# Mixture of experts: each expert's gate row brought to all partitions by a DMA instead of a bf16 product, and the first layer's products rotated over four PSUM banks

## The reference, cut to what matters

```python
shared = gelu(x @ sW1 + sb1) @ sW2 + sb2                  # one shared expert, 512 hidden units
weights = softmax(x @ gW + gb)                            # 15 experts
topv, topi = top_k(weights, 3)
gated = (one_hot(topi, 15) * topv[..., None]).sum(-2)     # 15 gates per token, 12 of them zero
routed = einsum('ebtd,bte->btd', expert_e(x), gated)      # 15 experts, 256 hidden units each
out = shared + routed + x
```

## Time and profile before

| | value |
|---|---|
| median of three runs | 2175.12 us |
| profiled execution, its own time | 2172.97 us |
| its span in the trace | 2171.2 us |
| PE busy | 1942.1 us, 89% of the span |
| DVE busy | 1490.1 us, 69% |
| ACT busy | 1440.6 us, 66% |
| POOL busy | 1137.4 us, 52% |
| experts' chunks in the trace | 419 to about 891 us |
| all DMA over the span | 29.16 MB |

### The profile page before, as it was taken

The page is one execution under the profiler, slowest core; times in us unless marked ns, Lnnn a source line. Parts: engine busy times, 40 slices in busy tenths (PEclk is TensorE's granted clock), DMA queues, the critical chain, the costliest instruction groups (busy, mean ns, idle before and its releaser), DMA issues. The chain is left out here.

```text
span 2171.2 us, 63152 instructions
## 1 busy us (share of the span) xinstructions
PE 1942.1 (89%) x23942; PEld 1524.2 (70%) x23942; DVE 1490.1 (69%) x3891; ACT 1440.6 (66%) x4147; POOL 1137.4 (52%) x1477
## 2 busy tenths in 40 slices
PE   5899887399999999699969999966999999999898
PEld 2577565166666667466658888854888888888787
DVE  7699658476666555477746666657777777777567
ACT  4588645387777778488857777747666666666542
POOL 5676359377877788545422232207555445444420
PEclk9999969699999999899989999989999999999999
DMA  3000000300000000000010000010000000000101
GB/s 89 9 2 2 8 2 2 94 1 1 1 1 1 1 1 1 11 2 3 2 32 2 2 2 2 2 65 5 2 17 5 15 17 5 15 15 2 53 8 37
DMA packets 32730, 29.16 MB, mean 13 GB/s; under 512 B 5534, under 2 KB 30126, under 8 KB 32174
## 3 DMA queue, kind: packets, MB, share of 16 engines
q1 hardware_dynamic: 23214, 20.93, 3.2%
q10 hardware_dynamic: 9216, 4.20, 0.7%
HBM read 20.92 MB, written 4.19 MB: 12 GB/s over the span
## 5 line engine op out<-in xcount | busy, mean ns | idle before, releaser
L1023 POOL TENSOR_TENSOR ff_hl<-ff_hid,ff_hh 128x512 fp32r<-128x512 f32 x272 | 353.9, 1309 | 115.5 <-ACT ff_hh L1262 109.0
L1877 POOL TENSOR_TENSOR sm_zsum<-sm_zsum,sm_logits 128x512 f32<-128x512 f32 x120 | 154.6, 1288 | 274.5 <-ACT sm_logits L1903 272.8
L1191 DVE TENSOR_TENSOR ff_hid<-ff_p_b,ff_hid 128x512 f32<-128x512 f32 x240 | 164.1, 685 | 157.7 <-ACT ff_hid L1251 157.4
L1251 ACT ACTIVATE ff_hid<-ff_p_h,ff_b 128x512 f32<-128x512 f32 x272 | 185.6, 683 | 49.5 <-PE ff_p_h L1079 48.1
L1920 ACT ACTIVATE sm_sT<-sm_p_s 128x512 f32<-128x512 f32 x128 | 69.5, 595 | 220.5 <-PE sm_p_s L1713 220.5
L1262 ACT ACTIVATE ff_hh<-ff_hid 128x512 fp32r<-128x512 f32 x272 | 170.1, 625 | 40.1 <-DVE ff_hid L1191 38.0
L581 ACT ACTIVATE at_pr<-at_p_s,at_small 128x64 f32<-128x64 f32 x512 | 154.8, 329 | 61.9 <-DVE at_small L469 61.9
L1889 POOL TENSOR_TENSOR sm_logits<-sm_logits,sm_peak 128x512 f32<-128x512 f32 x128 | 163.0, 1295 | 12.7 <-ACT sm_comb L1938 12.1
L1727 PE MATMUL sm_p_l<-g_phi,g_xnT 128*128 128x256 f32 x512 | 142.6, 405 | 26.8 <-ACT sm_logits L1948 25.4
L548 POOL TENSOR_TENSOR at_kblk<-at_kT,at_heads 128x512 f32<-128x512 f32 x128 | 131.8, 1049 | 35.0 <-PE at_p_s L448 23.6
L1077 PE MATMUL ff_p_h<-ff_xh,ff_w1h 128*128 128x512 f32 x272 | 135.0, 496 | 12.3 <-ACT ff_hid L1251 8.5
(11 more groups left out here) (316 smaller groups left out, 5738.5 us busy)
## 6 DMA issues: line engine op xcount, KB each, us to landing
sm_w<-in_w_soft SPq DMA_DIRECT2D x8, 512.0 KB, 3.5
ff_whole<-in_L_ffn_rW SPq DMA_DIRECT2D x30, 128.0 KB, 2.5
early_xs<-in_x ACTq DMA_DIRECT2D x32, 64.0 KB, 1.9
ld_ctx<-in_ctx ACTq DMA_DIRECT2D x32, 64.0 KB, 2.0
x_kept<-early_xs SPq DMA_DIRECT2D x1, 2048.0 KB, 7.4
g_xnT<-x_kept SPq DMA_DIRECT2D x1, 2048.0 KB, 9.2
out_x<-sm_acc SPq DMA_DIRECT2D x8, 256.0 KB, 2.3
g_phi<-in_L_ffn_phi SPq DMA_DIRECT2D x8, 128.0 KB, 2.4
```

The costliest lines, as they stand in the source:

```text
L1023: eng.tensor_tensor(hl[:, q, :], hid[:, q, :], hh[:, q, :].bitcast(F32), ALU.subtract).then_inc(h_split, 1)
L1191: dve.tensor_tensor(h, p_b[e % 2][:, :], h, ALU.mult).then_inc(scaled, 1)
L1251: act.activation(hid[:, slot(u, c), :], p_h[c % 2][:, :], ACT.Gelu, bias=b1[:, c:c + 1]).then_inc(gelud, 1)
L1877: pool.tensor_tensor(z, z, logits[:, j % RING_L, :, :], ALU.add).then_inc(summed, 1)
```

## The change

It has two parts. First, the gates no longer pass through bf16 parts, PE and PSUM. The float32 gates `gT` of a group (15 rows of 512) are stored to a DRAM buffer by the SP queue, and SP then loads, for each expert, its row of 2 KB into all 128 partitions of one of five SBUF slots (`gates`, 256 KB a load). So the product L1068, the transpose and copy of the parts and the last five router steps are gone, the transpose of the gates moves from c = 30 to c = 21, and the multiply on DVE reads its gates from SBUF. SP waits in its own order: for `gT`, for the store, and before each load for the multiplies of the expert five before. Its loads for group 0 stand behind the second piece of weights. The constants lose `c_spread` and `c_identb`. Second, the two PSUM banks so freed go to `p_h`: product c waits for the Gelu of chunk c-4 instead of c-2.

```diff
@@ -945,11 +945,11 @@
+    GR, PH = 5, 4
+    gates_d = nc.dram_tensor("kept_gates", (NE, NT * P), F32, kind="Internal").ap()
...
-        spread = m.sb("spread", [P, NE, P], BF16)
-        identb = m.sb("identb", [P, P], BF16)
...
-        parts = m.sb("parts", [P, 4, P], BF16)
-        partsT = m.sb("partsT", [P, R, N], BF16)
+        gates = m.sb("gates", [P, GR, N])
...
-        p_h = [m.ps(f"p_h{i}") for i in range(2)]
-        p_b = [m.ps(f"p_b{i}") for i in range(2)]
+        p_h = [m.ps(f"p_h{i}") for i in range(PH)]
...
+        def spread_gates(sync, t, experts_of):
+
+            at = slice(t * N, (t + 1) * N)
+            if experts_of[0] == 0:
+                sync.wait_ge(gT_copied, t + 1)
+                sync.dma_start(gates_d[:, at], gT[0:NE, t % R, :]).then_inc(gates_kept, 16)
+                sync.wait_ge(gates_kept, 16 * (t + 1))
+            for e in experts_of:
+                n = NE * t + e
+                if n >= GR:
+                    sync.wait_ge(scaled, CE * (n - GR + 1))
+                sync.dma_start(gates[:, n % GR, :], gates_d[e:e + 1, at].to_broadcast([P, N])).then_inc(gate_in[n % GR], 16)
...
                 for dst, src in piece:
                     sync.dma_start(dst, src).then_inc(w_in[i], 16)
-
-
-        AT_LOGITS, AT_LOGITS_T, AT_PARTS_T, AT_G_T = 1, 3, 26, 30
+                if i == 1:
+                    spread_gates(sync, 0, range(GR))
+            spread_gates(sync, 0, range(GR, NE))
+            for t in range(1, NGR):
+                spread_gates(sync, t, range(NE))
+
+        AT_LOGITS, AT_LOGITS_T, AT_G_T = 1, 3, 21
...
@@ -1057,26 +1071,16 @@
-                        if c >= CS and (c - CS) % CE == 0:
-                            e = (c - CS) // CE
-                            if e == 0:
-                                pe.wait_ge(pT_copied, t + 1)
-                            if e >= 2:
-                                pe.wait_ge(scaled, (NC_FF - CS) * t + CE * (e - 1))
-                            elif live(t - 1):
-                                pe.wait_ge(scaled, (NC_FF - CS) * t)
-                            pe.matmul(p_b[e % 2][:, :], spread[:, e, :], partsT[:, u, :], start=True, stop=True).then_inc(b_done, 1)
-                        if c >= 2:
-                            pe.wait_ge(gelud, NC_FF * t + c - 1)
-                        elif live(t - 1):
-                            pe.wait_ge(gelud, NC_FF * t)
+                        n = NC_FF * t + c
+                        if n >= PH:
+                            pe.wait_ge(gelud, n - PH + 1)
...
-                    if c == AT_PARTS_T and nxt:
-                        pe.wait_ge(parts_ready, t + 2)
-                        for q in range(4):
-                            mm = pe.transpose(p_q[:, :].bitcast(BF16)[:, q * P:(q + 1) * P], parts[:, q, :], identb[:, :])
-                        mm.then_inc(pT_done, 1)
                     if c == AT_G_T and nxt:
-                        pe.wait_ge(pT_copied, t + 2)
+                        pe.wait_ge(r_step, STEPS * (t + 2))
...
@@ -1186,9 +1178,10 @@
                         dve.wait_ge(gelud, NC_FF * t + c + 1)
-                        dve.wait_ge(b_done, NE * t + e + 1)
+                        n = NE * t + e
+                        dve.wait_ge(gate_in[n % GR], 16 * (n // GR + 1))
                         h = hid[:, slot(u, c), :]
-                        dve.tensor_tensor(h, p_b[e % 2][:, :], h, ALU.mult).then_inc(scaled, 1)
+                        dve.tensor_tensor(h, gates[:, n % GR, :], h, ALU.mult).then_inc(scaled, 1)
...
@@ -1266,11 +1259,10 @@
-                    if c == AT_PARTS_T + 1 and nxt:
-                        act.wait_ge(pT_done, t + 2)
-                        act.activation(partsT[:, (u + 1) % 2, :], p_q[:, :].bitcast(BF16)[:, 0:N], ACT.Copy).then_inc(pT_copied, 1)
                     if c == AT_G_T + 1 and nxt:
                         act.wait_ge(gT_done, t + 2)
+                        if live(t - 1):
+                            act.wait_ge(gates_kept, 16 * t)
```

More of the change, by code:

```diff
@@ L959, in experts @@
         loads = [(gw[:, :], io["L0_ffn_gW"]), (gb[:, :], io["L0_ffn_gb"].rearrange("(e a) -> e a", a=1)),
-                 (spread[:, :, :], io["c_spread"].rearrange("p (e m) -> p e m", e=NE)), (identb[:, :], io["c_identb"]),
                  (seg[:, :], io["c_seg"]), (b1[:, :], io["w_b1"]), (b2[:, :], io["w_b2"])]
@@ L985, in experts @@
         s4 = m.sb("s4", [P, 5, 4])
-        parts = m.sb("parts", [P, 4, P], BF16)
-        partsT = m.sb("partsT", [P, R, N], BF16)
+        gates = m.sb("gates", [P, GR, N])
         gT = m.sb("gT", [NE + 1, R, N])
-        p_h = [m.ps(f"p_h{i}") for i in range(2)]
-        p_b = [m.ps(f"p_b{i}") for i in range(2)]
+        p_h = [m.ps(f"p_h{i}") for i in range(PH)]
         p_y, p_t, p_n, p_q = m.ps("p_y"), m.ps("p_t"), m.ps("p_n"), m.ps("p_q")
         consts_in, zeroed = m.sem("consts_in"), m.sem("zeroed")
-        w1_done, gelud, scaled, h_used, b_done = (m.sem(n) for n in ("w1_done", "gelud", "scaled", "h_used", "b_done"))
+        w1_done, gelud, scaled, h_used = (m.sem(n) for n in ("w1_done", "gelud", "scaled", "h_used"))
         y_done, y_copied, yt_done, x_made = (m.sem(n) for n in ("y_done", "y_copied", "yt_done", "x_made"))
-        q_done, q_copied, lg_done, r_step, r_exped, parts_ready = (
-            m.sem(n) for n in ("q_done", "q_copied", "lg_done", "r_step", "r_exped", "parts_ready"))
-        pT_done, pT_copied, gT_done, gT_copied = (m.sem(n) for n in ("pT_done", "pT_copied", "gT_done", "gT_copied"))
+        q_done, q_copied, lg_done, r_step, r_exped = (m.sem(n) for n in ("q_done", "q_copied", "lg_done", "r_step", "r_exped"))
+        gT_done, gT_copied, gates_kept = m.sem("gT_done"), m.sem("gT_copied"), m.sem("gates_kept")
+        gate_in = m.sems("gate_in", GR)
         norm = Norm(m, g, x_made)
@@ L1000, in experts @@
         first, last = -1, NGR + 1
-        STEPS = 22
+        STEPS = 18
         def live(k):
@@ L1045, in _ @@
             pe.wait_ge(consts_in, 16 * len(loads))
-            pe.wait_ge(zeroed, 3)
+            pe.wait_ge(zeroed, 2)
             def turn(t, u):
@@ L1076, in turn @@
                             pe.wait_ge(w_split, 2 * (piece_of(c) + 1))
-                        pe.matmul(p_h[c % 2][:, :], w1h[:, c, :], xh[:, u, :], start=True, stop=False)
-                        pe.matmul(p_h[c % 2][:, :], w1h[:, c, :], xl[:, u, :], start=False, stop=False)
-                        pe.matmul(p_h[c % 2][:, :], w1l[:, c, :], xh[:, u, :], start=False, stop=True).then_inc(w1_done, 1)
+                        pe.matmul(p_h[n % PH][:, :], w1h[:, c, :], xh[:, u, :], start=True, stop=False)
+                        pe.matmul(p_h[n % PH][:, :], w1h[:, c, :], xl[:, u, :], start=False, stop=False)
+                        pe.matmul(p_h[n % PH][:, :], w1l[:, c, :], xh[:, u, :], start=False, stop=True).then_inc(w1_done, 1)
                         if c == LAG and live(t - 1):
@@ L1136, in _ @@
             dve.memset(lgT[:, :], 0.0).then_inc(zeroed, 1)
-            dve.memset(parts[:, :, :], 0.0).then_inc(zeroed, 1)
             dve.memset(gT[:, :, :], 1.0).then_inc(zeroed, 1)
             dve.wait_ge(consts_in, 16 * len(loads))
-            dve.wait_ge(zeroed, 3)
+            dve.wait_ge(zeroed, 2)
             def turn(t, u):
@@ L1168, in turn @@
                     lambda: (step(17), dve.tensor_tensor(sel[:, :, :], wt[:, :, :], cum[:, :, :], ALU.mult).then_inc(r_step, 1)),
[L1170 to L1174, removed]
                 ]
@@ L1220, in _ @@
             act.wait_ge(consts_in, 16 * len(loads))
-            act.wait_ge(zeroed, 3)
+            act.wait_ge(zeroed, 2)
             def round_weights(i):
@@ L1250, in turn @@
                             wait_split(act, t, c - HR)
-                        act.activation(hid[:, slot(u, c), :], p_h[c % 2][:, :], ACT.Gelu, bias=b1[:, c:c + 1]).then_inc(gelud, 1)
+                        act.activation(hid[:, slot(u, c), :], p_h[(NC_FF * t + c) % PH][:, :], ACT.Gelu, bias=b1[:, c:c + 1]).then_inc(gelud, 1)
                     n, v, h = (t, u, c - BACK) if c >= BACK else (t - 1, (u - 1) % R, NC_FF - BACK + c)
@@ L2005, in shape_constants @@
     bf16 = mybir.dt.np(BF16)
-    spread = np.zeros((P, NE, P))
-    for e in range(NE):
-        spread[[e, NE + e, 2 * NE + e], e] = 1.0
-    c["c_spread"] = spread.reshape(P, NE * P).astype(bf16)
     c["c_identb"] = np.eye(P).astype(bf16)
```

## The result

| | before | after |
|---|---|---|
| median of the runs | 2173.48 us (4 runs beside those of after) | 2216.53 us (4 runs, 2215.88 to 2218.61) |
| profiled execution, its own time | 2172.97 us | 2216.86 us |
| its span in the trace | 2171.2 us | 2215.0 us |
| DVE busy | 1490.1 us | 1608.3 us |
| POOL busy | 1137.4 us | 1218.6 us |

The change makes the kernel slower: the ratio is 1.020, with a 95% interval of 1.018 to 1.022. The multiply is L1184 (L1191 before), POOL's subtraction L1020 (L1023), Gelu L1244, the rounding L1255, the first layer's products L1081 to L1083, the second layer's L1068 to L1070.

What follows compares the result with a forecast made beforehand. PE set the pace before; DVE and POOL in turns would become the bound. Eight groups' segments less seven turns gave +48 us, the start +1: 2222 us profiled, so 2224 us forecast, range 2190 to 2288.

Steps and rivals of the forecast that it cites:

- likeliest mechanism: In the experts' stage, DVE's multiply and POOL's subtraction, both on SBUF operands, take turns and become the bound; chance 0.72.
- 1.15 + 0.55 = 1.70 us: Time a gated chunk needs of POOL's subtraction plus DVE's multiply in turn, against 1.37 us of PE.
- Blocking for the whole of the other: Rival for the multiply and subtraction: whole durations add up, gated chunks at 1.97 us, 2287 us in all; chance 0.08.
- never overlap: Reading of the earlier trace: DVE and POOL instructions on SBUF operands take turns, the later ending 0.81 to 1.15 us after.
- 9 to 20: Segment from chunk 9 to 20 of a group, with router and norm steps: 24.5 us forecast against 19.81, +4.7.
- the four pairs of root steps: Term in chunks 9 to 20: POOL's root steps at 0.75 us a pair, 3.0 us added to the sum.
- 20 to 33: Segment from chunk 20 to 33 of a group: 13 x 1.70 = 22.1 us against 18.34, +3.8.
- 4 to 9: Segment from chunk 4 to 9, where table loads hold ACT: 9.0 us against 9.55, -0.5, bounds -1.0 and 0.
- 33 to 4: Turn to the next group, mostly without multiplies, PE up to two chunks ahead: 8.0 us against 10.29, -2.3.
- The start: Group 0: five gate loads before weights, against earlier gates and 480 KB fewer constants; +1 us, bounds -3 and +4.
- 28.8 + 17.6 = 46 us: Gain if nothing came in return: 120 gate products off PE, 28.8 us, and at most 17.6 from four banks.
- the faster rival: PE's relief is what shows, since DVE and POOL would hardly meet: -46 us, 2129 us; chance 0.14.

## Why the prediction was right

**The forecast** was 2224 us, the measurement 2216.5, slower as foreseen and inside the range of 2190 to 2288. The likeliest mechanism is the one that the runs show: the multiply at 1344 ns on average, POOL at 1588, PE and ACT waiting for them, no one for the loads. Its central number, 1.15 + 0.55 = 1.70 us for a pair, was measured at 1.706 in 11 intervals. The second SBUF operand alone (2228.89 us) and its removal (2148.54) bracket the effect from both sides. That the time came this near is in part luck: the segments miss by 0.5, -1.8, -1.0 and 1.2 us in their order and partly cancel, and about 4 us behind the last multiply, for which the sum had no term, make up for some of what it had too much.

**Blocking for the whole of the other** was the rival at 2287 us. By the Trainium skill, "SBUF — State Buffer", section "Who interferes with whom", a two-SBUF-input instruction on DVE contends with a GpSimd one that reads SBUF, one with at most one SBUF input does not (outside its two-port modes), and the shared port is held for the whole instruction. The trace agrees on the multiply, which contends with two inputs in SBUF and not with one (687 ns), but the pitch of 1.706 us lies 0.26 below the 1.97 us of whole durations. Behind the other's end the multiply needs 0.55 us and the subtraction 1.15, each some 0.13 less than its duration alone, so "never overlap" in the prediction was not exact; its sum used the right values.

**Segment by segment.** The period was forecast 1.2 us too long (63.6 against 62.43), which over eight groups is 9.4 of the 9.6 us between the 48 forecast and the 38.4 measured.

- *9 to 20*: +2.9 instead of +4.7. My sum called 23.4 us a floor, reached only if the two always hand over at once; 22.67 was measured, so it was none. Two rows of after show why, the first on POOL, the second on DVE.

```profile
519.56 0.55 POOL L266 TENSOR_TENSOR ff_n_rstd<-ff_n_rstd,g_neghalf 128x1 f32<-128x1 f32 x1
```

```profile
519.74 0.68 DVE L1184 TENSOR_TENSOR ff_hid<-ff_gates,ff_hid 128x512 f32<-128x512 f32 x1
```

  The multiply from 519.74 to 520.42 starts inside POOL's root step, which ends at 520.11, and still takes 0.68 us. I had added the four pairs of root steps, 3.0 us, as time lost to both; here one overlaps with a multiply. POOL's timeline from 511.93 to 535.22 us has both sides of it: the 12 subtractions take 1.44 us each on average and not 1.70, the four pairs of root steps 4.57 us and not 3.0, and POOL is idle for 1.42.
- *20 to 33*: +2.7 instead of +3.8. Thirteen steps at 1.70 are 22.1 us, but the run does not begin in turns. Its first multiply takes 0.68 us and the second starts 0.79 us after it, at 535.92; from 540.85 to 556.19 the nine steps are 1.70 us each.
- *4 to 9*: -0.1 instead of -0.5. ACT's table loads hold it as before.
- *33 to 4*: -1.1 instead of -2.3. I let PE enter the turn two chunks ahead because of its banks. With two banks the turn looks the same, so the shorter turn has another cause. That it is the order in which POOL and ACT work off what is left is an argument; no run took it apart.

Together 8 x (2.86 + 2.72 - 0.09) - 7 x 1.05 = 36.6 us, where 38.4 was measured from first to last multiply and 48 was forecast. The segments are read in one group, and the first and the last group differ from it.

**The start** was put at +1 and came out at +1.4, but by two larger terms that cancel, which is luck. Five loads ahead of the weights cost 6.9 us, read from the kernel with one load first (40.0 against 33.1 us from first weight load to first multiply). Everything else at the start won 5.5, since that kernel needs 33.1 us where before needed 38.6; that this is the earlier gates and the fewer constants was not tested. My bounds of -3 and +4 were too narrow for the first alone.

**The step that failed** is the relief of PE, "28.8 + 17.6 = 46 us" with "PE sets the pace". With the operand in PSUM the kernel wins 27 us over before, not 46. Of the 2.75 us that its period is shorter (55.24 against 57.99), 1.80 lie in chunks 20 to 33, 0.65 at the turn, 0.28 in chunks 4 to 9, and 0.02 from 9 to 20. There it was not PE that set the pace but DVE's short steps with two SBUF inputs beside POOL, as the earlier trace rows already showed: 216 ns alone, 1309 beside POOL. I used those rows to price the multiply and not to ask what bounded that segment. Where POOL is nearly out of the way, with its subtraction cut to 32 columns, the kernel does win over 46 us (2175.16 - 2121.81 = 53), so the relief exists and shows once the two engines no longer hold each other up. The forecast was not hurt, because PE has slack in it, but the faster rival was priced at 2129 us where its true value is about 2149.

## What to carry to other kernels

Before an operand of a DVE instruction moves from PSUM to SBUF, look whether it becomes the second SBUF input and whether GpSimd works beside it; if so, price it by the pair and not by DVE's own duration. The cheap cure is to leave the other input in PSUM, here by writing the Gelu back into its bank, and it serves small steps with two SBUF inputs too (1.3 us back to 0.2). A load that is well hidden in the steady state can still cost several microseconds where its queue brings in weights: issue there only what the first consumer needs.

## What the runs showed of the hardware

- The pair takes 1.706 us in lockstep, less than the two durations alone (0.68 + 1.29 us). A multiply then shows 1.44 us, or 1.78 where DVE is never idle between two of them, so most of its wait lies inside its own duration, and the trace names no releaser for it.
- A 128x1 root step on POOL does not hold up a 128x512 multiply with two SBUF inputs that starts 0.18 us after it (the multiply still takes 0.68 us), but is itself drawn out where the multiply is first (0.87 to 0.95 us): L266 takes 725 ns on average in this stage of after, 558 before.
- A 128x128 scale and shift on DVE from SBUF to SBUF (L273) takes 0.34 us alone and 1.08 beside POOL's subtraction.
- A 256 KB load that spreads a 2 KB row over 128 partitions takes 0.32 us to issue and lands in 3.0 to 3.1 us, about as long as a 256 KB load of weights (3.3). Of the five that go out together in group 0, the first takes 3.6 us and the last 9.5.
